# Up and down products of a gated FFN as pairs of 64-row products in two PSUM banks

## The reference

```
scale = cond @ norm_w.T + 1.0
ms = mean(x * x, axis=-1)
h = x * (scale[:, None, :] * rsqrt(ms + 1e-6))
u = h @ up_w.T
val, gate = split(u, 2, axis=-1)
h = val * gelu(gate)
hq = act_quant(h)        # per token: round(h * 127 / max|h|), back to float
wq = weight_quant(down_w)  # ternary, one scale for the matrix
y = hq @ wq.T
return y + x
```

## Time and profile before

| | |
|---|---|
| median of 3 runs | 426.65 us (426.52 to 426.77) |
| profiled execution | 426.46 us, its span 424.7 us |
| TensorE matmul busy | 420.3 us, 2089 matmuls |
| TensorE weight load busy | 337.4 us, 2089 loads |
| VectorE, ScalarE, GpSimd busy | 279.4, 187.9, 165.2 us |
| granted TensorE clock | 1.0 over the span |

### The profile page before, as it was taken

One profiled execution on the slowest core, in us unless ns is written; L12 is line 12 of the kernel. 1 busy time (PEld: TensorE's weight loads), 2 busy tenths in 40 slices (PEclk: granted clock), 3 DMA queues, 4 the chain that ended last, 5 costly groups with the idle time before them and its releaser, 6 DMA issues.

```text
span 424.7 us, 7679 instructions
## 1 busy us (share of the span) xinstructions
PE 420.3 (99%) x2089; PEld 337.4 (79%) x2089; DVE 279.4 (66%) x538; ACT 187.9 (44%) x335; POOL 165.2 (39%) x323
## 2 busy tenths in 40 slices
PE   8999999999999999999999999999999999999997
PEld 6778888888888788888888887888888888878786
DVE  4986656756657657567566576565675565765676
ACT  6764344444344443444443444434444434444541
POOL 2644443443434434434424344334344243343320
PEclk9999999999999999999999999999999999999999
DMA  8523444333443424443334434244433344342324
GB/s 271 203 54 111 115 99 121 101 79 94 123 99 99 115 71 111 99 121 102 80 93 124 99 100 119 67 109 99 123 99 78 95 124 99 100 120 68 83 51 125
DMA packets 82088, 45.01 MB, mean 106 GB/s; under 512 B 68256, under 2 KB 68768, under 8 KB 81952
## 3 DMA queue, kind: packets, MB, share of 16 engines
q1 hardware_dynamic: 81792, 44.60, 40.3%
q10 hardware_dynamic: 288, 0.33, 0.3%
HBM read 20.00 MB, written 8.39 MB: 67 GB/s over the span
## 4 chain that ended last, share of the span: by engine, by line
PE 96%; DMA 1%; DVE 1%; ACT 1%; SPq 0%; issue 0%; POOL 0%; DVEq 0%; POOLq 0%
PE p_gate L768 41%; PE p_val L768 41%; PE p_y L788 13%; DMA up_raw<-up_w_t 1%; DVE up_lo L487 0%; PE p_val L746 0%; ACT up_hi L376 0%; DVE y_sb L531 0%; PE p_val L752 0%; PE p_val L747 0%; PE p_gate L788 0%; SPq L223 0%; ACT gelu L386 0%; DVE h L496 0%; DVE y_sb L668 0%
## 5 line engine op out<-in xcount | busy, mean ns | idle before, releaser
L625 DVE SCALAR_TENSOR_TENSOR h<-p_val,rstd,gelu 128x512 f32<-128x512 f32 x124 | 92.4, 745 | 128.0 <-PE p_val L768 127.1
L426 ACT ACTIVATE gelu<-p_gate,rstd 128x512 f32<-128x512 f32 x124 | 84.9, 685 | 142.7 <-PE p_gate L768 135.6
L299 POOL TENSOR_TENSOR mean_sq_eps<-mean_sq,rms_eps 128x1 f32<-128x1 f32 x64 | 12.2, 190 | 234.2 <-ACT squares L360 234.2
L372 ACT ACTIVATE q<-q_rounded 128x1024 bf16<-128x1024 f32 x63 | 66.6, 1057 | 77.9 <-DVE q_rounded L592 77.9
L768 PE MATMUL p_gate<-up_hi,a_lo 128*128 128x512 f32 x248 | 80.6, 406 | 0.0
L768 PE MATMUL p_val<-up_hi,a_hi 128*128 128x512 f32 x248 | 78.2, 396 | 0.0
L768 PE MATMUL p_val<-up_hi,a_lo 128*128 128x512 f32 x248 | 78.1, 396 | 0.0
L768 PE MATMUL p_val<-up_lo,a_hi 128*128 128x512 f32 x248 | 78.1, 396 | 0.0
L768 PE MATMUL p_gate<-up_hi,a_hi 128*128 128x512 f32 x248 | 78.1, 396 | 0.0
L768 PE MATMUL p_gate<-up_lo,a_hi 128*128 128x512 f32 x248 | 78.1, 395 | 0.0
L578 DVE TENSOR_REDUCE h_max<-h 128x1 f32<-128x1024 f32 x63 | 76.5, 1215 | 1.2
(11 more groups left out here) (87 smaller groups left out, 250.0 us busy)
## 6 DMA issues: line engine op xcount, KB each, us to landing
xt_in<-x_t SPq DMA_DIRECT2D x32, 256.0 KB, 2.8
x_all<-x SPq DMA_DIRECT2D x32, 256.0 KB, 2.9
out<-y_sb SPq DMA_DIRECT2D x31, 256.0 KB, 2.0
up_raw<-up_w_t SPq DMA_DIRECT2D x7, 256.0 KB, 5.3
down_raw<-down_w_t SPq DMA_DIRECT2D x1, 1024.0 KB, 7.9
q_t<-q SPq DMA_TRANSPOSE x63, 3.1
up_raw<-up_w_t ACTq DMA_DIRECT2D x1, 256.0 KB, 2.9
out<-y_sb SPq DMA_DIRECT2D x1, 128.0 KB, 2.0
```

Source lines behind the costliest of these rows:

```text
L299: pool.tensor_tensor(mean_sq_eps[:, j:j + 1], mean_sq[:, j:j + 1], rms_eps[:, :], ALU.add).then_inc(pool_step, 1)
L372: act.activation(q[j % 2][:, :], q_rounded[j % 2][:, :], ACT.Copy, bias=-ROUND).then_inc(q_ready, 1)
L426: act.activation(gelu[c][:, :], p_gate[c][:, :], ACT.Gelu, scale=rstd[:, j:j + 1]).then_inc(gelu_done, 1)
L625: nc.vector.scalar_tensor_tensor(h[s][:, c * W:(c + 1) * W], p_val[c][:, :], rstd[:, j:j + 1], gelu[c][:, :], op0=ALU.mult, op1=ALU.mult). ...
```

## The change

Every up matmul of 128 contraction rows becomes two of 64. In `up(u, j, c, turn)`, the gate bank takes a product of partitions 0 to 63 and the value bank one of partitions 64 to 127, one after the other in the program; after six such pairs both banks hold half of their sum. In the second turn the banks change sides. The order in a tile is turn 0 of half 0, turn 0 of half 1, turn 1 of half 0, turn 1 of half 1. Gate and value banks of a half are now begun together and completed together.

The down product does the same with two tiles in two banks (`down_pair`); the four `p_y` banks now hold the four tiles of a unit, and a pair's first and second turn stand behind different tiles. The early products, the total of L815, and the tail from tile 58 on keep 128 rows.

```diff
-            def up(u, j, c):
+            def halves(turn):
+                return [(which, slice(0, P // 2) if which == turn else slice(P // 2, P)) for which in range(2)]
+
+            def up(u, j, c, turn):
                 t = UNIT * u + j
-                if c == 0:
-                    pe.wait_ge(a_ready, t - 1)
-                for which, bank, done, read in ((0, p_gate[c], gate_done, gelu_done), (1, p_val[c], val_done, h_done)):
-                    col = 2 * c + which
-                    pe.wait_ge(read, NP * (t - 1) + c + 1)
-                    products = [(a_lo[j], up_hi), (a_hi[j], up_lo), (a_hi[j], up_hi)]
-                    for n, (a, w) in enumerate(products):
-                        for k in range(KD):
-                            last = nc.tensor.matmul(bank[:, :], a[:, k, :], w[:, col, k, :],
...
+                if turn == 0:
+                    if c == 0:
+                        pe.wait_ge(a_ready, t - 1)
+                    pe.wait_ge(gelu_done, NP * (t - 1) + c + 1)
+                    pe.wait_ge(h_done, NP * (t - 1) + c + 1)
+                else:
+                    pe.wait_ge(up_turned, TPB * (NP * (t - 2) + c + 1))
+                banks = (p_gate[c], p_val[c])
+                products = [(a_lo[j], up_hi), (a_hi[j], up_lo), (a_hi[j], up_hi)]
+                steps = [(a, w, k) for a, w in products for k in range(KD)]
+                for n, (a, w, k) in enumerate(steps):
+                    for which, rows in halves(turn):
+                        product = nc.tensor.matmul(banks[which][:, :], a[rows, k, :], w[rows, 2 * c + which, k, :],
...
+            def down_pair(u, j, turn):
...
+                for k in range(KF):
+                    for which, rows in halves(turn):
+                        product = nc.tensor.matmul(p_y[j + which][:, 0:D], q_t[j + which][rows, k, :],
+                                                   down_t[rows, k, :], start=(turn == 0 and k == 0),
...
             def unit(u, first, last=False):
                 for j in range(TPB if first else 0, UNIT):
-                    up(u, j, 0)
-                    for n in range(downs_at(j, first, last)):
-                        down(u - 1, j + n)
+                    for turn in range(2):
+                        for c in range(NP):
+                            up(u, j, c, turn)
                     if first and j == TPB:
...
-                    up(u, j, 1)
+                    if not first and not last and j < UNIT - 1:
+                        turn = (j + 1) % 2
+                        down_pair(u - 1, TPB * ((j + 1) // 2), turn)
...
+                    if not last and j == UNIT - 1:
+                        down_pair(u, 0, 0)
...
-            for t in range(TAIL, TILES):
+            down_pair(UNITS - 2, 0, 1)
+            for t in range(TAIL + 1, TILES):
```

More of the change, by code:

```diff
@@ L162, in slot, with finished_at @@
             return (j + UNIT, 1) if isinstance(u, int) and u == UNITS - 1 else (j, u + 1)
[L164 to L168, removed]
+        def finished_at(j, first, last):
+            return not first and not last and j % TPB == 1
         def early(t, c):
@@ L253, in unit @@
                         transpose(u - 1, UNIT - 1)
-                    if j % TPB == 0 and not first and not last:
-                        store(u - 1, i)
                     if j % TPB == TPB - 1 and not last and not (first and j == 1):
@@ L261, in unit @@
                         load_x(u + 1, i)
+                    if j % TPB == 1 and not first and not last:
+                        store(u - 1, i)
             unit(0, True, False)
@@ L641, in unit @@
                                                     ALU.max).then_inc(last_step, 1)
-                        if downs_at(j, first, last) > c:
-                            finish(u - 1, j + c)
+                        if finished_at(j, first, last):
+                            finish(u - 1, j - 1 + c)
                     if last and j == UNIT - 1:
@@ L648, in unit @@
                     quantised(u, j, t)
-                    rescale(u, j)
+                    if last:
+                        rescale(u, j)
+                    elif j % TPB == 1:
+                        rescale(u, j - 1)
+                        rescale(u, j)
             unit(0, True)
@@ new lines, in down_pair @@
+            def down_pair(u, j, turn):
+                if turn == 0:
+                    for n in range(TPB):
+                        m, count = slot(u, j + n)
+                        pe.wait_ge(qt_landed[m], 16 * count)
+                else:
+                    pe.wait_ge(down_turned, UNIT * u + j + TPB)
+                for k in range(KF):
+                    for which, rows in halves(turn):
+                        product = nc.tensor.matmul(p_y[j + which][:, 0:D], q_t[j + which][rows, k, :],
+                                                   down_t[rows, k, :], start=(turn == 0 and k == 0),
+                                                   stop=(turn == 1 and k == KF - 1))
+                        if k == KF - 1:
+                            product.then_inc((down_turned, y_done)[turn], 1)
@@ L816, in unit @@
                                          stop=True).then_inc(total_done, 1)
-                    up(u, j, 1)
+                    if not first and not last and j < UNIT - 1:
+                        turn = (j + 1) % 2
+                        down_pair(u - 1, TPB * ((j + 1) // 2), turn)
+                    if first and j == UNIT - 1:
+                        pe.wait_ge(down_ready, 1)
+                    if not last and j == UNIT - 1:
+                        down_pair(u, 0, 0)
             first_gate()
```

17 lines of the change are left out of this document (11 added, 6 removed).

## The result

The changed kernel takes **433.22 us** (median of 3 runs, 432.89 to 433.72) against 426.65 us: slower, ratio 1.0154 (95% interval 1.0140 to 1.0167). The forecast was 431.8 us, in a range of 405 to 440. The profiled execution took 433.22 us with a span of 431.4 us, 6.76 us more than the span before of 424.66.

A forecast was written before the change was run, and what follows sets the result against it. TensorE's own stream bounds the kernel, matmuls busy 99% of the span. Terms 0.4 + 0.4 + 1.8 + 1.5 + 1.0 = 5.1 us on 426.46 give 431.6, plus 0.19 for the median: 431.8 us, range 405 to 440.

The forecast's parts named there:

- The slot: Up matmuls: 0.2333 us each because 512 four-byte columns are streamed, not because of weight loads; a pair costs the same.
- faster rival: Up pairs: half-height streams reach 0.218 us a slot, 22.8 us fall out, about 409 us; chance 0.22.
- Side by side: 64-row pairs: both halves run at the same time, so a pair costs one slot, 0.2333 us.
- Issue: Down pairs: 32 loads and matmuls can be issued in 0.88 us, 27 ns each, so the matmuls add 0.
- Visits: Down products, 4 visits per unit in place of 2: 28 more changes between kinds of matmul add 0.4 us (0 to 1).
- Changes of height: Four, into unit 0, around the total of L815, out of it, in the tail: some 0.1 each, 0.4 us (0 to 1).
- The loop's 0.29 us of room: Loop, half 1: stream possible at T + 3.24, wanted at T + 3.53, so 0.29 us to spare and no stalls.
- Last unit: Tiles 60 to 63, no covering down pair: three stalls of 0.60 us, together 1.8 (1.2 to 2.6).
- The signal gaps: Waits between engines, such as gelu to h and h to weight load: 0.05 us allowed for each signal.
- Unit 0: Tile 2 to 3: h of half 1 behind VectorE's work on the total; stalls of 1.5 us (1 to 2).
- Tail: Behind the last up matmul: last h 0.90 us later, second finish in VectorE's way; adds 1.0 us (0.5 to 1.4).
- the step that put the loss at the transposes: Tail: last q ends later, so the transposes, started at 419.26, could start at about 420.0, 0.75 us later.

The follow-up runs named there:

- one half alone: Changed kernel with the four middle pairs of each six-pair up turn issuing only one of their two products, down pairs whole: 436.18 us.
- The run with bf16 corrections: Kernel before, full height, with the two correction products of the main loop given bf16 operands: 411.58 us, ratio 0.9648.
- the full-height kernel with the same visits: Changed kernel's order and places, but up and down products at the full 128 rows: 427.83 us, ratio 1.0024.
- the version with bf16 halves: Changed kernel with the correction products in bf16, the kinds in reverse order in half 1: 419.46 us, ratio 0.9832.
- The early total: Changed kernel with the total of L815 between the turns of tile 2, VectorE's ternary step and rescales ahead of h of half 0: 433.25 us, ratio 1.0163.
- the run with the cover: Changed kernel with one down pair moved from the tail to behind tile 60, its two finishes in tile 61: 433.05 us, ratio 1.0155.
- 160 idle instructions: Changed kernel with ten satisfied waits ahead of each turn's up matmuls in the last unit: 433.40 us, ratio 1.0155.

## Why the prediction was right, step by step

- **The slot.** "The extra time belongs to streaming 512 four-byte columns": right. Pairs of the loop cost 0.2338 us; one half alone costs the same; two-byte operands cost 0.215 at either height. With this the faster rival (409 us) is excluded for its own reason: half height changes neither the columns nor their bytes. By the rule of the Trainium skill's page "TensorE: Matmul & The Clock Gate", section "The mechanism", that a load overlaps matmuls in flight only when the row group differs, a full-height slot would be long by its load. The run with bf16 corrections speaks against it once more, with full-height slots of 0.215 us whose loads are of the same rows. (The same section of the Trainium skill also lets a load into the background weight buffer be pulled ahead; no run here tells which case applies.)
- **Side by side.** Right, and it needs different rows: 825.89 us where the rows were the same.
- **Issue.** 32 instructions in 0.89 us held, as the earlier trace rows had it; with bf16 up products too (0.87).
- **Visits.** 0.4, measured 0.46; over tiles 8 to 59 0.42, and 0.51 in the full-height kernel with the same visits.
- **Changes of height.** 0.1 each, measured 0.13 where there are many; the one into unit 0 is 0.19, by tile 2 of the changed kernel (5.79) against that of the full-height kernel in its order (5.60).
- **The loop's 0.29 us of room.** Right: no wait in the loop. In the version with bf16 halves the room was smaller and still held.
- **Last unit.** 1.8, measured 2.29, within its bounds of 1.2 to 2.6. The place and the count were right. The signal gaps were read from one early stall (0.05 each) and were 0.11 to 0.13 here.
- **Unit 0.** 1.5 and two height changes, measured 1.91. The early total took the stall away and so confirmed its cause.
- **Tail.** 1.0 (0.5 to 1.4) and a change of height, measured 1.90: the one term outside its bounds. Two things failed. First, the step that put the loss at the transposes; the finish of tile 56 in front of them bound first, and the chain named in the prediction came only second, as the run with the cover shows. Second, 0.75 us of store issue were in no term: the longer code of TensorE was counted as issue slots and never as bytes to be fetched. TensorE's own part, 1.15, was inside the bounds.

The sum was 5.1 us on the profiled execution and is 6.76: the tail's excess makes 0.8, the last unit's 0.5, unit 0's 0.2, the start's and the loop's the rest. The 0.19 that the prediction added for the median over the profiled execution did not come back: in the changed kernel the two are equal.

Two sums in the prediction are off, and nothing hangs on them. The tail has 48 slots ahead of the last tile's product, 8 of pairs and 40 full ones, and not 56; before it had 48, too. And the upper bounds of its terms add up to 8.0 us, which gives 434.7 and not 436; 433.22 lies below both.

## What to carry to other kernels

Splitting a matmul's contraction in two side by side shortened nothing where the array was already full: here the price was set by the columns streamed and their bytes, so look for columns or bytes to save, as the bf16 correction products did for 15 us. What such a split changes is when banks are completed. Count for each bank the time from completion to reuse, separately where the covering work is missing (first and last unit, tail); there the loss was 6.1 of 6.8 us (0.75 of it the held-up store), while the 56 tiles of the loop lost 0.5.

## What was not expected of the hardware

- Changing between full and half height costs 0.13 us a time beside another kind of matmul (15.1 us in 114 changes), more than a pair of down matmuls (0.11); between four-byte and two-byte matmuls at equal height a block of six with such a change takes 1.32 or 1.34 us, where four slots of 0.215 and two of 0.233 make 1.33.
- Longer code of one engine showed as a slower DMA issue on another: 1.1 to 1.55 us in place of 0.4 at the last stores, each time with a 16 KB fetch of TensorE's code beside it, and each held-up issue of over 1 us in the thirteen traces ended 0.36 to 0.40 us behind the fetch. Where such a fetch falls moved with 160 idle instructions, so edits worth 1 us near the end of a kernel can be masked by it.
- The five runs of the changed kernel spread over 2.2 us and the eight of the kernel before beside them over 0.7. Why is open.
